# A two-layer graph attention network on one core: destination rows spread into PSUM by TensorE, lane numbers and softmax weights read from SBUF by VectorE

## The chip, the cores and the metric

The kernel runs on one core of one Trainium2 chip. The metric is the device time of one execution in microseconds (us), lower is better; the number quoted for a kernel is the median of several executions.

## What is computed

Two layers of graph attention over N = 3125 nodes with D = 128 features, E = 100,000 edges sorted by destination, H = 8 heads of 16, and a feed-forward network of width 512 after each attention. Cut to what matters:

```
for l in range(2):
    xn  = layernorm(x);  xp = xn + xn @ Wpos + bpos + deg * Wdeg + bdeg
    q, k, v = xp @ Wq + bq, xp @ Wk + bk, xp @ Wv + bv
    att = clip((q[dst] * k[src]).sum(head) / 4, -50, 50)      # one number per edge and head
    alpha = softmax of att over the edges (and the self loop) of each dst
    x = x + segment_sum(v[src] * alpha, dst) @ Wo + bo
    x = x + gelu(layernorm(x) @ W1 + b1) @ W2 + b2
out = layernorm(x_in + x)
```

## The kernel before

The nodes lie in 25 tiles of 128. The edges are cut into 99 groups a layer: 97 of 1024 edges (8 chunks of 128), and two short ones. Groups are worked from the last destinations to the first, so early groups can touch two tiles or more; a layer has 123 pairs of a group and a tile, 246 in both layers, against 198 groups. A group whose edges fall in two tiles is called doubled below. All five engines run the same loop over groups, each in its own program order, and meet through counting semaphores:

- **POOL** fetches the key and value rows of a group's source nodes, one indirect DMA a chunk (L561), into `kv`, which has 4 slots (`SLOTS`). Before group g it waits for `sum_begun` of the group that used the slot last. Its 8 gathers of a group are called a burst below.
- **SP** loads the destinations of each group, 1024 int32 broadcast to all 128 partitions (512 KB), into `dst_rows`, which has 3 slots (`ROWS`; L490). Before each it waits for `exp_done`.
- **ACT** makes the transposed one-hot matrix `hotT` of each pair, two groups ahead: `dist` = |destination - lane's node| from `dst_rows` (L697), `hotT` = relu(1 - dist) in bf16 (L700, which waits for `hotT_used`, posted by the gather's last matmul). It also takes the exponentials of the scores, once into `msg` (L706) and once more into the PSUM tile `shares` (L707). In its program the exponentials of group g stand ahead of the one-hots of group g + 2.
- **PE** (TensorE) gathers the queries of group g + 1 by `hotT` into PSUM banks 0 and 1: 24 bf16 matmuls for each pair (`gather_q`, L1332; it waits for `prod_done` of group g and `hotT_ready`). Then it sums the messages of group g by destination: 8 fp32 products for each pair, which the trace shows as 16 matmuls (`sum_pair`, L1350, into bank 2). The first product of a group posts `sum_begun`, the last of a pair `agg_done`.
- **DVE** (VectorE) makes `hot`, the one-hot matrix that is not transposed, from the destinations and 128 lane numbers in the PSUM tile `lanes` (L987), multiplies keys and queries (`prod`, L1069), sums them by head (`dots`, L1079), clips (L1081 to L1084), multiplies values by `shares` into `msg` (L1101), and adds each tile's sum to `acc` (L982).

In groups 36 to 83 of each layer the engines also carry out 24 "slots" of the feed-forward network, one for every two groups. The order on every engine is written out by hand; the number of pairs in a group is read at run time from `pair_tab`, and a loop (`Fori`) runs over them. PSUM has 8 banks: 0 and 1 hold the queries, 2 the sum, 3 `lanes`, 4, 5 and 6 the slots' tiles, 7 `shares`.

## Time and profile before

| what | us |
|---|---|
| median of 3 executions | 2742.39 |
| lowest and highest | 2732.53 and 2750.9 |
| the profiled execution | 2747.29 |
| its span in the trace | 2745.3 |
| busy in that span: PE, DVE, POOL, ACT | 1663.2, 1452.9, 1487.1, 912.1 |

The profile is a page for one execution (busy time of the engines, the chain of work that ended last, the costliest groups of instructions) and views of the trace that it was made from: groups by line with the idle time before them, the waits, and a timeline of instructions. In all of them "<-" behind an idle time names what released the instruction; "remote" is a semaphore whose poster the trace does not give, "issue" is time in which the engine waited for nothing that is shown.

### The profile page before, as it was taken

How to read it: one execution, taken by the hardware profiler on the slowest of the kernel's cores; microseconds unless marked ns; L12 is line 12 of the kernel's file. 1: busy time of each engine (PE TensorE's matmuls, PEld its weight loads, DVE VectorE, ACT ScalarE, POOL GpSimd, SP SyncE). 2: the span in 40 equal slices, each digit the busy share in tenths (PEclk: the TensorE clock that was granted, in tenths of full speed). 3: DMA queues.
4: the chain of work that ended last, by engine and by line, in shares of the span. 5: the costliest groups of instructions: out<-in, count | busy, mean ns of one | idle time of the engine just before them, and what ended most of it. 6: DMA issues, size and time to landing. Idle time of an engine off the chain costs nothing.

```text
span 2745.3 us, 44122 instructions
## 1 busy us (share of the span) xinstructions
PE 1663.2 (61%) x11693; PEld 1456.9 (53%) x11694; DVE 1452.9 (53%) x2484; ACT 912.1 (33%) x1616; POOL 1487.1 (54%) x1584
## 2 busy tenths in 40 slices
PE   7555555656666767666544565555656666665645
PEld 5454554555555656554533454555555555655644
DVE  9654444445555555555464444445455555555544
ACT  3223222223443444343232222222333443433422
POOL 0445555555555555556635555555655555655663
PEclk9668777667887777778566777767787777777776
DMA  2433334344433434444423333333433333443443
GB/s 67 132 108 121 112 109 125 115 121 122 125 115 116 127 115 127 124 123 141 132 79 104 120 106 119 117 117 120 131 119 119 117 117 117 123 128 117 129 136 93
DMA packets 120300, 322.97 MB, mean 118 GB/s; under 512 B 31459, under 2 KB 43684, under 8 KB 120170
## 3 DMA queue, kind: packets, MB, share of 16 engines
q0 software_dynamic: 75072, 205.10, 26.0%
q1 hardware_dynamic: 44292, 115.07, 12.5%
q10 hardware_dynamic: 838, 1.60, 0.2%
q8 instruction: 49, 0.80, 0.1%
q14 instruction: 49, 0.40, 0.0%
HBM read 313.45 MB, written 9.73 MB: 118 GB/s over the span
## 4 chain that ended last, share of the span: by engine, by line
DVE 25%; another core or an unknown queue 22%; issue 20%; PE 17%; DVEq 11%; ACT 3%; ACTq 1%; DMA 0%; SPq 0%
PE ps L1332 7%; PE ps L1350 6%; DVE dots L1079 6%; DVE prod L1069 5%; DVEq L354 4%; DVEq L388 3%; DVE hot L987 2%; DVE msg L1101 2%; DVE acc L982 1%; DVE q_parts L834 1%; DVEq L982 1%; DVE not_nan L1081 1%; DVEq L987 1%; ACT dist L697 1%
## 5 line engine op out<-in xcount | busy, mean ns | idle before, releaser
L561 POOL DMA_INDIRECT kv<-kv_tab,src_idx x1564 | 1483.3, 948 | 1230.9 <-PE ps L1350 541.0
L1350 PE MATMUL ps<-msg,hot 128*128 128x136 f32 x3896 | 764.3, 367 | 425.6 <-DVE acc L982 232.9
L1350 PEld LDWEIGHTS ps<-msg,hot 128*128 128x128 f32 x3896 | 705.6, 267 | 484.0 <-issue 298.0
L1332 PE MATMUL ps<-q_parts,hotT 128*128 x5844 | 560.0, 265 | 526.9 <-DVE prod L1069 228.5
L1332 PEld LDWEIGHTS ps<-q_parts,hotT 128*128 x5844 | 483.0, 121 | 610.7 <-issue 591.8
L1069 DVE TENSOR_TENSOR prod<-kv,ps 128x1024 f32<-128x1024 f32 (+1 forms) x198 | 238.2, 1203 | 362.1 <-remote 286.1
L987 DVE SCALAR_TENSOR_TENSOR hot<-dst_col,neg_base,ps 128x1024 f32<-128x1024 f32 (+1 forms) x246 | 311.7, 1267 | 126.1 <-issue 124.6
L700 ACT ACTIVATE hotT<-dist 128x1024 bf16 x246 | 259.9, 1057 | 331.2 <-remote 291.5
L697 ACT ACTIVATE dist<-dst_rows,neg_node 128x1024 bf16<-128x1024 int32 x246 | 282.5, 1148 | 153.0 <-issue 146.3
L1101 DVE TENSOR_TENSOR msg<-kv,ps 128x1024 f32<-128x1024 f32 (+1 forms) x198 | 238.7, 1205 | 105.5 <-issue 72.4
L706 ACT ACTIVATE msg<-att 128x64 f32<-128x64 f32 (+1 forms) x198 | 49.7, 251 | 625.9 <-DVE att L1084 468.9
L1079 DVE TENSOR_REDUCE dots<-prod 128x64 f32<-128x1024 f32 (+1 forms) x198 | 238.8, 1206 | 21.1 <-DVE prod L1069 14.9
L982 DVE TENSOR_TENSOR acc<-acc,ps 128x136 f32 x246 | 71.3, 290 | 295.4 <-PE ps L1350 166.2
L655 ACT ACTIVATE hid_slot<-ps,b1f 128x128 f32<-128x128 f32 x192 | 54.7, 368 | 309.5 <-PE ps L1303 201.4
L1303 PE MATMUL ps<-z1T,w1g 128*128 128x128 f32 x384 | 78.0, 356 | 52.1 <-issue 51.2
L1303 PEld LDWEIGHTS ps<-z1T,w1g 128*128 128x128 f32 x384 | 66.6, 255 | 63.1 <-issue 62.9
L638 ACT ACTIVATE spot<-spot,eps_col 128x1 f32<-128x1 f32 x100 | 29.0, 290 | 173.5 <-issue 92.8
L1019 DVE TENSOR_TENSOR x<-x,ps 128x128 f32<-128x128 f32 x26 | 7.4, 286 | 142.5 <-remote 110.4
L1309 PE MATMUL ps<-w,hid_slot 128*128 128x128 f32 x384 | 65.4, 325 | 16.1 <-ACT hid_slot L655 16.1
L1309 PEld LDWEIGHTS ps<-w,hid_slot 128*128 128x128 f32 x384 | 59.5, 236 | 18.7 <-ACT hid_slot L655 18.7
L667 ACT ACT_TABLE_LOAD x52 | 66.7, 1283 | 0.9
L664 ACT ACT_TABLE_LOAD x50 | 64.2, 1283 | 0.9
(215 smaller groups left out, 1000.8 us busy)
## 6 DMA issues: line engine op xcount, KB each, us to landing
dst_rows<-in_dst SPq DMA_DIRECT2D x194, 512.0 KB
kv<-kv_tab,src_idx POOLq DMA_INDIRECT x1564
kv_tab<-qkv SPq DMA_DIRECT2D x25, 128.0 KB
kv_tab<-qkv SPq DMA_DIRECT2D x3, 768.0 KB
out_tab<-z SPq DMA_DIRECT2D x24, 64.0 KB
out<-out_tab SPq DMA_DIRECT2D x1, 1498.5 KB
hot<-in_L_gnn_W SPq DMA_DIRECT2D x2, 256.0 KB
w<-in_L_gnn_W SPq DMA_DIRECT2D x2, 256.0 KB
```

The lines of the kernel that those rows point to most:

```text
L561: pool.indirect_dma_start(kv[:, u, c, :], None, kv_tab[l][:, :], bass.IndirectOffsetOnAxis(ap=src_idx[:, c, at(g)], axis=0)).then_inc(kv_i ...
L697: nc.scalar.activation(dist[:, :], dst_rows[:, r, :], ACT.Abs, bias=neg_node[:, at(t)]).then_inc(dist_done[l], 1)
L700: nc.scalar.activation(hotT[:, bass.ds(pr % 2, 1), :], dist[:, :], ACT.Relu, bias=1.0, scale=-1.0).then_inc(hotT_ready[l], 1)
L982: nc.vector.tensor_tensor(acc[:, at(t), :], acc[:, at(t), :], agg.unsqueeze(1), ALU.add).then_inc(evac_done[l], 1)
L987: nc.vector.scalar_tensor_tensor(out=hot[:, u % 2, 0:nch, :], in0=dst_col[:, 0:nch, at(g)].broadcast_to([P, nch, P]), scalar=neg_base[:, a ...
L1069: nc.vector.tensor_tensor(prod[:, 0:full].rearrange("p (c d) -> p c d", d=D), kv[:, u, 0:nch, 0:D], qd[:, 0:full].rearrange("p (c d) -> p ...
L1079: nc.vector.tensor_reduce(dots[:, 0:scores], prod[:, 0:full].rearrange("p (n d) -> p n d", d=HD), AX.X, ALU.add).then_inc(dot_done[l], 1)
L1101: nc.vector.tensor_tensor(half[:, 0:nch, 0:D].rearrange("p c (h d) -> p c h d", d=HD), kv[:, u, 0:nch, D:2 * D].rearrange("p c (h d) -> p ...
L1303: last = MM(banks["h"][c], w1g[:, l, c * P:(c + 1) * P], z1T[s], start=True, stop=True)
L1309: MM(banks["y"], hid[s][:, c * P:(c + 1) * P], w2[:, l, c, :], start=(c == 0), stop=False)
L1332: last = MM(qd[:, c * P:(c + 1) * P], hotT[:, bass.ds(pr % 2, 1), c * P:(c + 1) * P], q_parts[:, at(t), k * D:(k + 1) * D], start=first an ...
L1350: last = MM(agg, hot[:, u % 2, c, :], msg[:, u % 2, c, :], start=(c == 0), stop=(c == nch - 1))
```

## The change

The destinations no longer come as a broadcast of 512 KB. Once, at the start, ACT copies the table of destinations (99 rows of 1024) to bf16, POOL subtracts that from the table, which gives the rest as a second exact bf16 number, and SP stores both parts to a table in DRAM. For each group SP then loads 2 rows of bf16, 4 KB, into `part_rows` (4 slots). PE adds the two parts and spreads them over all partitions with two matmuls against a matrix of ones (`spread_row`, 2x128 by 2x512, one for each of the PSUM banks 3 and 4). It stands in PE's program after `gather_q` of group g + 1 and ahead of the sums, works for group g + 2, and waits for the row and for `dist_done` of all pairs of group g + 1, since the banks hold one row. ACT's `dist` reads the banks and waits for `rows_spread`.

DVE's `hot` reads the lane numbers from the SBUF tile that they were copied from, and `msg` takes the weights from the SBUF tile `msg` itself; the second exponential is gone. Both instructions now have two tensor inputs in SBUF, where they had one in SBUF and one in PSUM. The slots' tiles that lay in bank 4 move to bank 7.

```diff
-ROWS = 3
-TURN = 2 * ROWS
+ROWS = 4
+TURN = 6
...
-        dst_rows = sb("dst_rows", [P, ROWS, GE], I32)
+        dst_parts = sb("dst_parts", [NG, 2, GE], BF16)
+        part_rows = sb("part_rows", [2, ROWS, GE], BF16)
+        both = sb("both", [2, P], BF16)
...
-        lanes = ps[:, 3, 0:P]
-        shares = ps[:, 7, 0:GC * H].rearrange("p (c h) -> p c h", h=H)
+        spread_rows = ps[:, 3:5, :]
...
-                   "y": bank(6, P), "z2T": bank(4, P), "qkv": bank(4, 3 * D)}
+                   "y": bank(6, P), "z2T": bank(7, P), "qkv": bank(7, 3 * D)}
...
+            sp.wait_ge(parts_done, 2)
+            sp.dma_start(part_tab[:, :, :], dst_parts[:, :, :]).then_inc(parts_out, 16)
...
                     if g >= ROWS:
-                        sp.wait_ge(exp_done[l], max(1, g - ROWS))
+                        sp.wait_ge(rows_spread[l], g - ROWS + 1)
                     elif l:
-                        sp.wait_ge(exp_done[l - 1], NG)
-                    first, n = edges_of(g)
-                    sp.dma_start(dst_rows[:, r, 0:n], dst_d[first:first + n].partition_broadcast(P)).then_inc(rows_in[l][r], 16)
+                        sp.wait_ge(rows_spread[l - 1], NG)
+                    elif g == 0:
+                        sp.wait_ge(parts_out, 16)
+                    sp.dma_start(part_rows[:, r, :], part_tab[NG - 1 - g, :, :]).then_inc(rows_in[r], 16)
...
+            pool.memset(both[:, :], 1.0).then_inc(consts, 1)
+            pool.wait_ge(parts_done, 1)
+            nc.gpsimd.tensor_tensor(dst_parts[:, 1, :], dst_f, dst_parts[:, 0, :], ALU.subtract).then_inc(parts_done, 1)
...
+            act.wait_ge(src_rows, 2)
+            nc.scalar.activation(dst_parts[:, 0, :], dst_f, ACT.Copy).then_inc(parts_done, 1)
...
-                    act.wait_ge(rows_in[l][r], 16 * (n + 1))
+                    act.wait_ge(rows_spread[l], g + 1)
...
-                        nc.scalar.activation(dist[:, :], dst_rows[:, r, :], ACT.Abs, bias=neg_node[:, at(t)]).then_inc(dist_done[l], 1)
+                        nc.scalar.activation(dist[:, :].rearrange("p (b e) -> p b e", b=2), spread_rows, ACT.Abs, bias=neg_node[:, at(t)]).then_inc(dist_done[l], 1)
...
-                    nc.scalar.activation(msg[:, u % 2, 0:nch, D:MW], scores, ACT.Exp, scale=1.0 / SCALE)
-                    nc.scalar.activation(shares[:, 0:nch, :], scores, ACT.Exp, scale=1.0 / SCALE).then_inc(exp_done[l], 1)
+                    nc.scalar.activation(msg[:, u % 2, 0:nch, D:MW], scores, ACT.Exp, scale=1.0 / SCALE).then_inc(exp_done[l], 1)
...
-                link(nc.vector.tensor_copy(lanes, lane_row[:, :]))
...
-                                                   scalar=neg_base[:, at(t)], in1=spread(lanes, 1, nch),
+                                                   scalar=neg_base[:, at(t)], in1=spread(lane_row[:, :], 1, nch),
...
-                                            spread(shares[:, 0:nch, :], 3, HD), ALU.mult).then_inc(msg_done[l], 1)
+                                            spread(half[:, 0:nch, D:MW], 3, HD), ALU.mult).then_inc(msg_done[l], 1)
...
+                def spread_row(u, g, n, before):
+
+                    r = u % ROWS
+                    pe.wait_ge(rows_in[r], 16 * (l * rows_of_lane(r) + n + 1))
+                    if not (isinstance(g, int) and g == 0):
+                        pe.wait_ge(dist_done[l], before)
+                    for h in range(2):
+                        last = MM(spread_rows[:, h, :], both[:, :], part_rows[:, r, h * (GE // 2):(h + 1) * (GE // 2)], start=True, stop=True)
+                    last.then_inc(rows_spread[l], 1)
...
                     if more:
                         gather_q(u + 1, g + 1, word(d)[0], *word(d + 1))
+                    if more > 1:
+                        spread_row(u + 2, g + 2, i + (u + 2) // ROWS, word(d + 1)[0])
                     if not (isinstance(g, int) and g == 0):
                         sum_further(u + 1, g - 1, word(d - 2)[0], word(d - 1)[0])
...
+                if l == 0:
+                    pe.wait_ge(tab_ready, 1)
+                    spread_row(0, 0, 0, 0)
                 pe.wait_ge(q_part[2], l * NU + NU)
+                if l:
+                    spread_row(0, 0, 0, 0)
                 gather_q(0, 0, word(-1)[0], *word(0))
+                spread_row(1, 1, 0, word(0)[0])
```

On PE, between the gather of a group's queries and the sum, the program before reads (the end of the loop over a group's further tiles, then the first sum):

```order
L1332 MATMUL ps<-q_parts,hotT 128x128 x3
L1338 REGISTER_ALU
L1338 COMPARE_AND_BRANCH
L1337 UNCONDITIONAL_BRANCH
L1350 MATMUL ps<-msg,hot 128x136 [waits evac_done0,hot_done0,msg_done0]
L1350 MATMUL ps<-msg,hot 128x136 x7
```

and the changed program at the same place:

```order
L1357 MATMUL ps<-q_parts,hotT 128x128 x3
L1363 REGISTER_ALU
L1363 COMPARE_AND_BRANCH
L1362 UNCONDITIONAL_BRANCH
L1344 MATMUL ps<-part_rows,both 128x512 [waits dist_done0,rows_in2]
L1344 MATMUL ps<-part_rows,both 128x512
L1375 MATMUL ps<-msg,hot 128x136 [waits evac_done0,hot_done0,msg_done0]
L1375 MATMUL ps<-msg,hot 128x136 x7
```

The two matmuls at L1344 are the spreading of the row two groups on; they stand ahead of the sum of the current group. On ACT, from a group's exponentials to the one-hots of the second group after it, the program before reads:

```order
L706 ACTIVATE msg<-att 128x8x8 [waits att_done0]
L707 ACTIVATE ps<-att 128x64
L354 TENSOR_LOAD pair_tab
L354 ISA x2
L694 ISA [waits rows_in0_2]
L694 UNCONDITIONAL_BRANCH
L694 ISA
L697 REGISTER_ALU [waits hotT_ready0]
L697 REGISTER_ALU
L697 ISA
L697 ACTIVATE dist<-dst_rows,neg_node 128x1024
L700 ISA [waits hotT_used0,dist_done0]
```

and the changed program:

```order
L723 ACTIVATE msg<-att 128x8x8 [waits att_done0]
L359 TENSOR_LOAD pair_tab
L359 ISA x2
L711 ISA [waits rows_spread0]
L711 UNCONDITIONAL_BRANCH
L711 ISA
L714 REGISTER_ALU [waits hotT_ready0]
L714 REGISTER_ALU
L714 ISA
L714 ACTIVATE dist<-ps,neg_node 128x1024
L717 ISA [waits hotT_used0,dist_done0]
L717 ACTIVATE hotT<-dist 128x1024
```

The wait at the head of the one-hots is for PE (`rows_spread`) where it was for a DMA (`rows_in`), and the activation into PSUM is gone.

## Rows read from the trace of the kernel before

**Rows 1.** The page's chain that ended last, share of the span by engine.
```profile
DVE 25%; another core or an unknown queue 22%; issue 20%; PE 17%; DVEq 11%; ACT 3%; ACTq 1%; DMA 0%; SPq 0%
```
**Rows 2.** The page's costliest groups: out<-in xcount | busy us, mean ns | idle before.
```profile
L561 POOL DMA_INDIRECT kv<-kv_tab,src_idx x1564 | 1483.3, 948 | 1230.9 <-PE ps L1350 541.0
...
L1069 DVE TENSOR_TENSOR prod<-kv,ps 128x1024 f32<-128x1024 f32 (+1 forms) x198 | 238.2, 1203 | 362.1 <-remote 286.1
L987 DVE SCALAR_TENSOR_TENSOR hot<-dst_col,neg_base,ps 128x1024 f32<-128x1024 f32 (+1 forms) x246 | 311.7, 1267 | 126.1 <-issue 124.6
L700 ACT ACTIVATE hotT<-dist 128x1024 bf16 x246 | 259.9, 1057 | 331.2 <-remote 291.5
L697 ACT ACTIVATE dist<-dst_rows,neg_node 128x1024 bf16<-128x1024 int32 x246 | 282.5, 1148 | 153.0 <-issue 146.3
```
**Rows 3.** Timeline of a steady group, layer 0: start us, us, engine, line, [idle before].
```profile
1363.17 0.94 POOL L561 DMA_INDIRECT kv<-kv_tab,src_idx  x1 [2.17 <-remote]
...
1364.71 2.80 PE L1332 MATMUL ps<-q_parts,hotT 128*128 x24 [3.86 <-DVE prod L1069]
...
1366.71 1.22 DVE L1101 TENSOR_TENSOR msg<-kv,ps 128x1024 f32<-128x1024 f32 x1 [0.72 <-ACT ps L707]
1366.92 0.95 POOL L561 DMA_INDIRECT kv<-kv_tab,src_idx  x1 [0.30 <-issue]
...
1368.05 1.27 DVE L987 SCALAR_TENSOR_TENSOR hot<-dst_col,neg_base,ps 128x1024 f32<-128x1024 f32 x1
...
1368.28 3.97 PE L1350 MATMUL ps<-msg,hot 128*128 128x136 f32 x16 [0.77 <-DVE acc L982]
...
1371.92 0.95 POOL L561 DMA_INDIRECT kv<-kv_tab,src_idx  x1 [0.30 <-issue]
1374.67 1.22 DVE L1069 TENSOR_TENSOR prod<-kv,ps 128x1024 f32<-128x1024 f32 x1 [5.34 <-remote]
1374.94 0.94 POOL L561 DMA_INDIRECT kv<-kv_tab,src_idx  x1 [2.08 <-remote]
```
**Rows 4.** Timeline at the start of layer 1, ACT.
```profile
1469.10 1.06 ACT L700 ACTIVATE hotT<-dist 128x1024 bf16 x1 [23.09 <-remote]
```
**Rows 5.** Timeline at the end of layer 0, POOL, around the 4-chunk group.
```profile
1390.52 0.95 POOL L561 DMA_INDIRECT kv<-kv_tab,src_idx  x1 [0.30 <-issue]
...
1392.92 0.94 POOL L561 DMA_INDIRECT kv<-kv_tab,src_idx  x1 [1.46 <-PE ps L1350]
```
**Rows 6.** Timeline between the layers: gathers beside DVE operations with two SBUF inputs.
```profile
1439.23 0.82 DVE L961 TENSOR_TENSOR q_parts<-acc,q_parts  x1 [0.72 <-issue]
1439.63 1.24 POOL L561 DMA_INDIRECT kv<-kv_tab,src_idx  x1 [0.30 <-issue]
...
1442.13 0.82 DVE L967 TENSOR_TENSOR acc<-qkv,acc  x1 [2.07 <-issue]
1442.43 1.35 POOL L561 DMA_INDIRECT kv<-kv_tab,src_idx  x1 [0.30 <-issue]
```
**Rows 7.** Timeline of a doubled group, layer 0.
```profile
389.18 5.25 PE L1332 MATMUL ps<-q_parts,hotT 128*128 x47 [5.54 <-ACT hotT L700]
...
394.82 0.22 PE L1332 MATMUL ps<-q_parts,hotT 128*128 x1 [0.39 <-issue]
...
396.37 0.95 POOL L561 DMA_INDIRECT kv<-kv_tab,src_idx  x1 [0.30 <-issue]
...
399.40 1.06 ACT L700 ACTIVATE hotT<-dist 128x1024 bf16 x1 [6.59 <-remote]
...
404.28 0.94 POOL L561 DMA_INDIRECT kv<-kv_tab,src_idx  x1 [6.97 <-PE ps L1350]
```
**Rows 8.** Groups by line: the second exponential, its reader, and wide bf16 matmuls.
```profile
L1101 DVE TENSOR_TENSOR msg<-kv,ps 128x1024 f32<-128x1024 f32 (+1 forms) x198 | 238.7, 1205 | 105.5 <-issue 72.4 <-ACT ps L707 32.6
...
L707 ACT ACTIVATE ps<-att 128x64 f32<-128x64 f32 (+1 forms) x198 | 41.2, 208 | 0.0
...
L1285 PE MATMUL ps<-q_parts,zeros 128*128 128x384 bf16 x48 | 14.6, 461 | 3.8 <-issue 3.8
```

More of the change, by code:

```diff
@@ L256, in gnn_program @@
         hot_used = sem("hot_used")
-        rows_in = [sems(f"rows_in{l}_", ROWS) for l in range(L)]
+        rows_in = sems("rows_in", ROWS)
+        rows_spread = sems("rows_spread")
+        parts_done = sem("parts_done")
+        parts_out = sem("parts_out")
         dst_away = sem("dst_away")
@@ L342, in gnn_program @@
         block = ctx.enter_context(nc.Block())
-        NCONST = 14
+        NCONST = 15
         RAW_LOADS = 16
@@ L712, in _, with edge_group @@
                 word = pair_words(act, 0)
-                one_hots(word, 0, 0, 0)
+                one_hots(word, 0, 0)
                 if l == 0:
                     fold_kept(1)
-                one_hots(word, 1, 1, 0)
-                def edge_group(word, d, g, u, r, n, slot=None):
+                one_hots(word, 1, 1)
+                def edge_group(word, d, g, u, slot=None):
                     even, odd = (slot is not None and u % 2 == k for k in (0, 1))
@@ L752, in _ @@
                     for u in range(TURN):
-                        edge_group(word, u, TURN * i + u, u, (u + 2) % ROWS, TURN // ROWS * i + (u + 2) // ROWS, slot=number + u // 2)
+                        edge_group(word, u, TURN * i + u, u, slot=number + u // 2)
                 word = pair_words(act, 0)
                 for g in range(2 * SLOT_END, NG):
-                    edge_group(word, g, g, g, (g + 2) % ROWS, (g + 2) // ROWS, slot=slot_at(g))
+                    edge_group(word, g, g, g, slot=slot_at(g))
                 start = tail_start(act)
@@ L1364, in tail_biases, with pe_group @@
                     MM(in_tail["y"], ones[0:1, :], b2_row[:, l, :], start=True, stop=False)
-                def pe_group(u, g, word, d, more=True, slot=None):
+                def pe_group(u, g, i, word, d, more=2, slot=None):
                     even, odd = (slot is not None and u % 2 == k for k in (0, 1))
@@ L1401, in _ @@
                     for u in range(SLOTS):
-                        pe_group(u, SLOTS * i + u, word, u)
+                        pe_group(u, SLOTS * i + u, i, word, u)
                 word = pair_words(pe, 0)
                 for g in range(2 * FIRST_SLOT, 2 * FIRST_SLOT + SLOTS):
-                    pe_group(g % SLOTS, g, word, g, slot=slot_at(g))
+                    pe_group(g % SLOTS, g, g // SLOTS, word, g, slot=slot_at(g))
                 with pe.Fori(2 * FIRST_SLOT // SLOTS + 1, 2 * SLOT_END // SLOTS) as i:
@@ L1409, in _ @@
                     for u in range(SLOTS):
-                        pe_group(u, SLOTS * i + u, word, u, slot=number + u // 2)
+                        pe_group(u, SLOTS * i + u, i, word, u, slot=number + u // 2)
                 word = pair_words(pe, 0)
                 for g in range(2 * SLOT_END, 2 * SLOT_END + SLOTS):
-                    pe_group(g % SLOTS, g, word, g, slot=slot_at(g))
+                    pe_group(g % SLOTS, g, g // SLOTS, word, g, slot=slot_at(g))
                 with pe.Fori(2 * SLOT_END // SLOTS + 1, NG // SLOTS) as i:
@@ L1416, in _ @@
                     for u in range(SLOTS):
-                        pe_group(u, SLOTS * i + u, word, u)
+                        pe_group(u, SLOTS * i + u, i, word, u)
                 word = pair_words(pe, 0)
                 for g in range(NG // SLOTS * SLOTS, NG):
-                    pe_group(g % SLOTS, g, word, g, more=g < NG - 1)
+                    pe_group(g % SLOTS, g, g // SLOTS, word, g, more=NG - 1 - g)
                 sum_further(NG - 1, NG - 1, word(NG - 2)[0], word(NG - 1)[0])
```

15 lines of the change are left out of this document (9 added, 6 removed).

## The prediction

> **What bounds the kernel now.** I read the chain that ended last first. It gives no engine more than a quarter: 25% VectorE, 22% "another core or an unknown queue", 20% issue, 17% PE [rows 1]. So several engines take turns around one loop, and semaphores whose poster is not shown hold it for a fifth of the time. Next I read the costliest groups for who waits [rows 2]: POOL's gathers are busy 1483.3 us and stood idle for 1230.9 before them, 541.0 of it for the sum on PE; `prod` waited 286.1 and `hotT` 291.5 for "remote". Then the timeline of one steady group, which shows what the loop is [rows 3]. POOL's burst begins at 1363.17 and its last gather at 1371.92, 8.75 us later. PE gathers queries at 1364.71 and sums from 1368.28 to 1372.25. Yet `prod`, which waits for the gather that was recorded by 1367.51, starts at 1374.67, and the next burst, which waits for the first product of a sum, starts at 1374.94. Both come 2.75 and 3.02 us after the burst's last issue. I read this as: while POOL issues a burst, PE's completions are not passed on; they arrive together some 1.8 us after the last gather ended. The start of layer 1 says the same without a row load under way: `hotT` waited 23.09 us for a gather recorded long before [rows 4]. The period, 1374.94 - 1363.17 = 11.77 us, is therefore a burst of 8.75 plus 3.02, and PE's and ACT's work is free as long as it ends inside it. A longer burst is paid in full.
>
> In a doubled group this cover is gone [rows 7]. PE runs 47 of the gather's 48 matmuls by 394.43, then single ones, while POOL still issues; the burst's last issue is at 396.37, the posts come at 399.40, and the next burst starts at 404.28, 7.91 us after the last issue instead of 3.02. There are 246 - 198 = 48 further pairs in the two layers, from the counts of `hot` and `prod` [rows 2].
>
> **The change part by part**, on the profiled execution (2747.29 us, 4.9 above the median).
>
> *VectorE's two operands in SBUF.* I expect no gain for VectorE: the instruction's element count stays. The loss is on POOL. Before, `msg` runs from 1366.71 to 1367.93 with one input in PSUM; a gather starts in the middle of it and still takes 0.95 [rows 3]. Where the operation beside it has two SBUF inputs, it is different [rows 6]: the gather that starts at 1439.63, inside L961 (1439.23 to 1440.05), takes 1.24, which is 0.95 counted from 0.13 before L961's end; the one at 1442.43, inside L967 (1442.13 to 1442.95), takes 1.35, by the same rule to 0.01. So a gather waits for the end of such an operation. In the steady group the gather at 1366.92 would wait for `msg` until 1367.80, 0.88 us, and the next, moved from 1368.17 to 1369.05, for `hot` (1368.05 to 1369.32) until 1369.19, 0.14: 1.02 us per burst, as an upper end 198 x 1.02 = +202. In other groups the two operations fall partly behind the burst; by the same two steps for each burst of the timeline, 325 of the 444 operations (246 + 198) hold the start of a gather, at 0.42 us on average: +136, my value. Lower end 0, if a gather needs the port only outside these pieces.
>
> A sentence of the Trainium skill bears on this from both sides: the page "SBUF — State Buffer", section "Who interferes with whom", states that a VectorE instruction with two SBUF inputs contends with a GpSimd instruction that reads SBUF, and one with at most one does not. By that the trace agrees, 1.24 and 1.35 against 0.95. The same section infers that descriptor generation needs only the write side, so that `tensor_tensor` would not stall a gather; by that the term were 0, and the two long gathers speak against it. It is a rival below.
>
> *The row's way over PE.* `dist` of group g + 2 may now start only when PE's post has arrived. In a steady group it arrives with the others at 1374.67: `dist` 1.15 and `hotT` 1.06 [rows 2] with 0.3 between end at 1377.2, and `prod`, for which the next gather waits too, at 1375.89 [rows 3]; of the 1.3 between I take half, 0.7, as the gather's delay, since PE needs a while after `prod` too. Behind it stand two matmuls of 512 columns. Their price: 24 matmuls of 128 columns took 2.80 [rows 3], 0.117 each, so 0.47 for 512 columns; L1285's 384 columns at 461 ns [rows 8] make 0.61 for 512, the upper end. Two cost 0.93. The sum would end 1.6 later, at 1373.9, and the posts come at 1374.7 + 1.0 for the longer burst: still hidden, 0.
>
> In a doubled group it is not hidden. The second pair's `dist` and `hotT` too stand behind the post, and the exponential of the group waits behind them on ACT's queue, with `msg` and the sum behind that. I take 0.7 for the late gather and 0.93 for the two matmuls: 1.6 us, 48 x 1.6 = +77. Lower end 0 (the trickle of single matmuls hides it); upper end two pairs' one-hots in full, 2 x 2.2 = 4.4, 48 x 4.4 = +211.
>
> In the 96 groups with slots (48 a layer) PE also has the feed-forward matmuls, and I take half of the two matmuls as exposed: 96 x 0.45 = +43, between 0 and 96 x 0.93 = +89. The slots' tiles that move to bank 7 cost nothing: `shares` is gone from it.
>
> *The second exponential.* 198 at 208 ns are 41.2 us, and `msg` waited 32.6 for it [rows 8]. `msg` starts earlier by less than its 0.21, and in steady groups only hidden work is shortened. I take half, -20, between -41 and 0.
>
> *Row loads.* 194 broadcasts of 512 KB go (97 whole groups a layer), 4 KB come. If that traffic were part of what delays the posts, the short burst at the layer's end, where no load is under way, bounds it: from its last issue at 1390.52 to the next burst at 1392.92 are 2.40 us [rows 5] against 3.02 in rows 3, so at most 198 x 0.62 = -123. Rows 4 show the long hold without any load, so I take 0.
>
> *Starts of the layers and prologue.* The first one-hots were ready before the posts came; now `spread`, `dist`, `hotT`, gather come after them, about 2.2 + 2.8 = 5 us a layer: +10, between 0 and +20. The table's copy, subtraction and store lie beside the preparation of nodes and tables and get no term of their own.
>
> Sum: 136 + 77 + 43 - 20 + 0 + 10 = +246. 2747.3 + 246 = 2993; less 4.9 for the median, 2988.
>
> **Rivals.**
> *Only the bursts count.* The chain over PE and ACT stays hidden in doubled and slot groups as well. For it: PE's single matmuls at the end of a burst are waiting time that extra work may fill. Against it: 7.91 us from the last issue to the next burst in a doubled group, with PE busy. Then 136 - 20 + 10 = +126: 2868.
> *No price at the port.* The page's inference holds for gathers, and the long ones of rows 6 have another cause. Then 77 + 43 - 20 + 10 = +110: 2852.
> *The loads were part of the hold* (the other side). Without 194 x 512 KB = 99 MB of writes into SBUF the posts come earlier after each burst. At 0.62 us a burst it is -123 and, with the chain then hidden, +126 - 123 = +3: 2745, no change; if the hold vanished, 1.8 us a burst, 198 x 1.8 = -356 and 2742 + 126 - 356 = 2512. It decides the sign from 0.64 us a burst on, 126 / 198. For it: the short burst of rows 5. Against it: rows 4, and that the short burst's sum starts late for its own reasons.
> *The chain cascades.* Port at the steady group's 1.02 (+202), doubled groups at 3 us (+144), slot groups at 0.93 (+89), -20 and +10: +425, 3167.
>
> **How the numbers follow.** Chances: forecast 0.50, only the bursts 0.20, no price at the port 0.07, loads 0.11, cascade 0.12. The first two rivals lie near each other and inside the range; the forecast's own range is 2900 to 3080. From 2810 to 3110 leaves out the loads' case and half of the cascade, some 0.18. A measurement of this kernel tells about 1% from no change. The loads' case I split into 0.07 faster and 0.04 within 1%; all others are slower by more, 0.89.
>
> **What would show it.** Port: mean time of a gather 0.948 [rows 2] rises to about 1.035 (136 / 1564 = 0.087), with single gathers of 1.1 to 1.9 that start inside `msg` or `hot`, and bursts of 9.2 to 9.8 instead of 8.75. Chain: `dist` idle before it for "remote" or PE, where it was 153.0 mostly issue; a doubled group some 2 us longer; gather matmuls that wait for `hotT`. Steady groups: period 12.8 instead of 11.77. VectorE's `msg` and `hot` keep 1205 and 1267 ns; if they became longer, VectorE and not POOL pays for the port, and the bursts would stay 8.75. The forecast is wrong if bursts stay at 8.75, if the posts come less than 2.4 us after a burst's last issue, or if steady groups too run longer than the burst explains.

## The result: 1.7% slower, not 9%

The changed kernel took 2788.8 us (median of 4, 2782.1 to 2802.0) where the kernel before took 2746.1 beside it (median of 4). The ratio is 1.0168, with a 95% interval from 1.0142 to 1.0193. The forecast was 2988 with a range from 2810 to 3110: the sign was right, the size was nearly six times too large, and the time lies below the range.

The profile after. The page's chain that ended last, share of the span by engine:

```profile
another core or an unknown queue 24%; PE 24%; issue 22%; DVE 13%; ACT 9%; DVEq 6%; ACTq 3%; DMA 0%; SPq 0%
```

Its costliest groups, columns as in [rows 2]:

```profile
L576 POOL DMA_INDIRECT kv<-kv_tab,src_idx x1564 | 1605.6, 1027 | 1141.2 <-PE ps L1375 497.0
...
L714 ACT ACTIVATE dist<-ps,neg_node 128x1024 bf16<-128x1024 f32 x246 | 273.9, 1113 | 1101.9 <-remote 754.3
L1002 DVE SCALAR_TENSOR_TENSOR hot<-dst_col,neg_base,lane_row 128x1024 f32<-128x1024 f32 (+1 forms) x246 | 313.0, 1272 | 235.1 <-issue 127.8
...
L1116 DVE TENSOR_TENSOR msg<-kv,msg 128x1024 f32<-128x1024 f32 (+1 forms) x198 | 240.4, 1214 | 114.9 <-issue 73.6
...
L1344 PE MATMUL ps<-part_rows,both 2*128 2x512 bf16 x396 | 161.2, 492 | 48.4 <-issue 26.8
```

Much of this stands as the prediction had it. The gather rose from 948 ns [rows 2] to 1027, which is 1605.6 - 1483.3 = 122 us more on POOL (136 was forecast). `hot` and `msg` keep their length, 1272 and 1214 against 1267 and 1205, so it is POOL that waits at the port, not VectorE. The wide matmul takes 492 ns, against my 0.47 us. And `dist`, which had waited 153.0 us before [rows 2], now waits 1101.9, mostly for a post of PE. Yet the idle time ahead of the gathers fell by 90 us, from 1230.9 to 1141.2: what the port added to the bursts was taken from the gaps between them.

The timeline of a steady group of the changed kernel shows how:

```profile
1321.13 0.94 POOL L576 DMA_INDIRECT kv<-kv_tab,src_idx  x1 [2.03 <-remote]
...
1324.75 1.23 DVE L1116 TENSOR_TENSOR msg<-kv,msg 128x1024 f32<-128x1024 f32 x1 [0.25 <-issue]
1324.88 1.91 POOL L576 DMA_INDIRECT kv<-kv_tab,src_idx  x1 [0.30 <-issue]
...
1330.85 0.94 POOL L576 DMA_INDIRECT kv<-kv_tab,src_idx  x1 [0.30 <-issue]
1332.85 1.22 DVE L1084 TENSOR_TENSOR prod<-kv,ps 128x1024 f32<-128x1024 f32 x1 [4.50 <-remote]
1333.17 0.95 POOL L576 DMA_INDIRECT kv<-kv_tab,src_idx  x1 [1.38 <-remote]
```

The gather at 1324.88 starts inside `msg` and takes 1.91 us; the last issue is 9.72 us after the first instead of 8.75. But `prod` starts 11.72 us after the first issue, where it was 1374.67 - 1363.17 = 11.50 [rows 3], and only 2.00 us after the last one, where it was 2.75; less than 2.4 was one of the prediction's own signs of being wrong. The posts did not move with the end of the burst. I had read a fixed distance from the last issue out of bursts that all had the same length, and from those the first issue fits just as well. The start of layer 1 in the trace of before had the answer. There four bursts run one behind the other; the first and the last of their 32 gathers:

```profile
1423.64 0.94 POOL L561 DMA_INDIRECT kv<-kv_tab,src_idx  x1 [28.53 <-DMA kv_tab<-qkv]
...
1464.09 0.95 POOL L561 DMA_INDIRECT kv<-kv_tab,src_idx  x1 [0.30 <-issue]
```

The post came at 1469.10 [rows 4]. That is 5.0 us after the last issue, not 2.75 to 3.02, and 45.5 us after the first, 1.42 for each of 32 gathers; 11.50 for 8 gathers are 1.44 each. I call this theory S: the posts wait for some work that takes 1.43 us a gather from the first issue on, so POOL's issues, 1.25 apart, have slack. Theory P is the prediction's: the posts come at a fixed distance from the last issue.

Where the 43 us lie in these two traces is seen by cutting both at `prod` of groups 4, 36, 84 and 96 of each layer. Of before, the rows read: stretch, its length, then busy time of PE, PEld, DVE, ACT and POOL, PE's granted clock, DMA share, GB/s.

```profile
193.24:613.61 420.37, 239.83 (x1771) 217.90 (x1772) 199.83 (x284) 108.91 (x152) 233.79 (x249) 0.73 0.39 117
613.61:1256.91 643.30, 428.99 (x2911) 369.90 (x2909) 354.91 (x661) 260.57 (x511) 362.72 (x384) 0.76 0.40 122
1256.91:1393.34 136.43, 76.77 (x503) 67.36 (x504) 70.29 (x105) 35.68 (x60) 86.81 (x93) 0.67 0.43 128
1524.33:1944.70 420.37, 239.89 (x1771) 217.72 (x1772) 199.64 (x283) 108.91 (x152) 233.83 (x249) 0.74 0.39 117
1944.70:2579.53 634.83, 407.13 (x2844) 359.64 (x2843) 348.68 (x662) 256.07 (x487) 362.45 (x383) 0.76 0.40 122
```

The same stretches of the changed kernel:

```profile
200.76:645.27 444.51, 264.98 (x1841) 217.81 (x1840) 200.80 (x283) 102.12 (x120) 254.67 (x249) 0.72 0.25 74
645.27:1284.73 639.46, 459.31 (x3004) 370.91 (x3003) 357.12 (x660) 247.98 (x459) 391.10 (x383) 0.76 0.29 84
1284.73:1422.65 137.92, 81.87 (x517) 64.35 (x516) 70.81 (x103) 33.42 (x49) 97.25 (x92) 0.69 0.31 91
1553.99:1998.76 444.77, 267.73 (x1840) 223.13 (x1840) 200.69 (x283) 102.29 (x120) 252.84 (x249) 0.70 0.26 74
1998.76:2622.66 623.90, 452.53 (x2934) 373.13 (x2934) 350.57 (x661) 243.42 (x437) 395.52 (x383) 0.74 0.29 83
```

Groups 4 to 35, without feed-forward slots, grew by 24.1 and 24.4 us. Groups 36 to 83, with slots, shrank by 3.8 and 10.9, although PE has 30 and 45 us more to do in them. The steady groups 84 to 95 grew by 1.5 in layer 0 and by 0.1 in layer 1. Of the rest, some 8 us, 7.5 lie ahead of `prod` of group 4 of layer 0 (200.76 against 193.24), although POOL's first gather starts no later there (86.28 against 86.53); the start of layer 1 grew by 0.4. A second pair of traces, in experiment 2, puts the cost elsewhere, so this table doesn't place it.

### The profile page after: what moved, and what is told of

The parts are those of the page before. It is cut to its first block, busy times and chain, and to the rows that moved or that the text cites. A ratio compares the mean times of both kernels' runs of the same rounds, so it can differ in the third digit from the quotient of the medians.

```text
span 2788.9 us, 44946 instructions
## 1 busy us (share of the span) xinstructions
PE 1817.7 (65%) x12089; PEld 1480.0 (53%) x12090; DVE 1460.3 (52%) x2482; ACT 871.6 (31%) x1419; POOL 1611.7 (58%) x1586
## 4 chain that ended last, share of the span: by engine, by line
another core or an unknown queue 24%; PE 24%; issue 22%; DVE 13%; ACT 9%; DVEq 6%; ACTq 3%; DMA 0%; SPq 0%
PE ps L1357 10%; PE ps L1375 8%; ACT dist L714 4%; DVE dots L1094 3%; DVE prod L1084 2%; DVEq L359 2%; PE ps L1344 2%; ACT hotT L717 2%; DVE q_parts L850 1%; ACTq L359 1%; DVE hot L1002 1%; PE ps L1318 1%; DVE msg L1116 1%; DVEq L397 1%
## 5 line engine op out<-in xcount | busy, mean ns | idle before, releaser
L576 POOL DMA_INDIRECT kv<-kv_tab,src_idx x1564 | 1605.6, 1027 | 1141.2 <-PE ps L1375 497.0
L1357 PE MATMUL ps<-q_parts,hotT 128*128 x5844 | 585.8, 271 | 570.0 <-issue 277.0
L1375 PE MATMUL ps<-msg,hot 128*128 128x136 f32 x3896 | 754.6, 364 | 246.4 <-DVE acc L997 138.0
L1375 PEld LDWEIGHTS ps<-msg,hot 128*128 128x128 f32 x3896 | 691.1, 262 | 369.5 <-issue 231.3
L1357 PEld LDWEIGHTS ps<-q_parts,hotT 128*128 x5844 | 500.9, 123 | 662.9 <-issue 643.3
L714 ACT ACTIVATE dist<-ps,neg_node 128x1024 bf16<-128x1024 f32 x246 | 273.9, 1113 | 1101.9 <-remote 754.3
L1002 DVE SCALAR_TENSOR_TENSOR hot<-dst_col,neg_base,lane_row 128x1024 f32<-128x1024 f32 (+1 forms) x246 | 313.0, 1272 | 235.1 <-issue 127.8
L1116 DVE TENSOR_TENSOR msg<-kv,msg 128x1024 f32<-128x1024 f32 (+1 forms) x198 | 240.4, 1214 | 114.9 <-issue 73.6
L1344 PE MATMUL ps<-part_rows,both 2*128 2x512 bf16 x396 | 161.2, 492 | 48.4 <-issue 26.8
L1344 PEld LDWEIGHTS ps<-part_rows,both 2*128 2x128 bf16 x396 | 25.3, 99 | 87.5 <-issue 81.3
```

The source lines that it names most:

```text
L576: pool.indirect_dma_start(kv[:, u, c, :], None, kv_tab[l][:, :], bass.IndirectOffsetOnAxis(ap=src_idx[:, c, at(g)], axis=0)).then_inc(kv_i ...
L714: nc.scalar.activation(dist[:, :].rearrange("p (b e) -> p b e", b=2), spread_rows, ACT.Abs, bias=neg_node[:, at(t)]).then_inc(dist_done[l], 1)
L1002: nc.vector.scalar_tensor_tensor(out=hot[:, u % 2, 0:nch, :], in0=dst_col[:, 0:nch, at(g)].broadcast_to([P, nch, P]), scalar=neg_base[:, a ...
L1116: nc.vector.tensor_tensor(half[:, 0:nch, 0:D].rearrange("p c (h d) -> p c h d", d=HD), kv[:, u, 0:nch, D:2 * D].rearrange("p c (h d) -> p ...
L1344: last = MM(spread_rows[:, h, :], both[:, :], part_rows[:, r, h * (GE // 2):(h + 1) * (GE // 2)], start=True, stop=True)
L1357: last = MM(qd[:, c * P:(c + 1) * P], hotT[:, bass.ds(pr % 2, 1), c * P:(c + 1) * P], q_parts[:, at(t), k * D:(k + 1) * D], start=first an ...
```

## The experiments

Each experiment was timed in turn with the kernel before on the same chip, and the ratios are to that. The time of the kernel before was not the same in all sets of runs, and this turned out to be the main finding: in two sets (that of experiment 2 with the repetition of experiment 1 and the long pause of experiment 4, and the last run of experiment 6) it took 2669 to 2671 us, in all others 2100 to 2105; beside the changed kernel's first measurement it had been 2746. One chip showed both, 2671 in one set and 2100 in a later one, so it is not a property of the chip alone. The two conditions are told apart by the trace, below, and I call them "held" (2669 to 2746 for the kernel before, which the prediction and the result are about) and "not held" (2100).

**Experiment 1: VectorE's two SBUF operands alone, on the kernel before.**

```diff
-                                                   scalar=neg_base[:, at(t)], in1=spread(lanes, 1, nch),
+                                                   scalar=neg_base[:, at(t)], in1=spread(lane_row[:, :], 1, nch),
...
-                                            spread(shares[:, 0:nch, :], 3, HD), ALU.mult).then_inc(msg_done[l], 1)
+                                            spread(half[:, 0:nch, D:MW], 3, HD), ALU.mult).then_inc(msg_done[l], 1)
...
-                    nc.scalar.activation(msg[:, u % 2, 0:nch, D:MW], scores, ACT.Exp, scale=1.0 / SCALE)
-                    nc.scalar.activation(shares[:, 0:nch, :], scores, ACT.Exp, scale=1.0 / SCALE).then_inc(exp_done[l], 1)
+                    nc.scalar.activation(msg[:, u % 2, 0:nch, D:MW], scores, ACT.Exp, scale=1.0 / SCALE).then_inc(exp_done[l], 1)
```

> The kernel before with only VectorE's part of the change: hot and msg read two SBUF operands, the second exponential and the copy of the lane numbers are gone; rows still come by the 512 KB broadcast. Theory P (the prediction's: the posts come about 3.0 us after a burst's last issue, so a longer burst is paid in full): gathers of 1.03 us on average, bursts of about 9.4, and +136 - 20 = +116, about 2860. Theory S (formed on the trace of after: the posts come about 11.5 us after a burst's FIRST issue, 1.43 us for each of 8 gathers, however late the last is issued): the same gathers and bursts, but the time between burst start and prod stays 11.5 to 11.7 in steady groups, and the kernel is within 1% of before, 2725 to 2775.

Measured: 2234.5 us against 2105.3, ratio 1.0626 (1.0598 to 1.0654), +129 us. Neither theory had said that before would take 2105. The difference is near theory P's +116, but not for P's reason: no post is held here, POOL simply issues without a pause, and what it pays is the longer gathers (1618.9 us of them, against 1484.7 in experiment 3, whose gathers are those of before). So this set doesn't decide between P and S. The same edit in a held set:

> The kernel before with VectorE's two SBUF operands alone, again, beside the changed kernel. Without hold: +129 as in the first set, and the changed kernel within 5 us of it. With hold: 0 to +15, and the changed kernel 30 to 50 above it.

Measured: 2669.5 against 2669.5, ratio 1.000 (0.997 to 1.003). So one edit costs 129 us or nothing, and which of the two depends on the condition. P's +116 is refuted for the held condition. The other half of S's expectation, `prod` 11.5 to 11.7 us after a burst's first issue, came true only in part. I take the 24 steady groups 84 to 95 of both layers. In this held trace `prod` starts 11.3 to 12.1 us after the first issue in 9 of them, and in 12 it starts before the burst's last issue; in the first profile of before these were 23 and 1, in the changed kernel 11 and 8. So with stalls inside the bursts some posts get through before a burst is over, which S as I put it did not have. The gathers are long in both. The page's row for them, not held and then held:

```profile
L561 POOL DMA_INDIRECT kv<-kv_tab,src_idx x1564 | 1618.9, 1035 | 580.6 <-issue 468.9
```
```profile
L561 POOL DMA_INDIRECT kv<-kv_tab,src_idx x1564 | 1604.8, 1026 | 1001.2 <-issue 428.3
```

1035 and 1026 ns, against 948 before. Not held, POOL's idle time is 580.6, and 468.9 of it is the 0.30 us between two gathers, so hardly anything is left to take a longer gather from, and the chain that ended last is POOL's:

```profile
POOL 65%; issue 21%; PE 5%; DVE 5%; DMA 3%; DVEq 1%; ACT 0%; ACTq 0%; POOLq 0%; SPq 0%
```

The timeline of one group, not held, with the stall that the prediction described:

```profile
1063.03 1.22 DVE L1099 TENSOR_TENSOR msg<-kv,msg 128x1024 f32<-128x1024 f32 x1 [1.07 <-ACT msg L706]
1063.24 1.84 POOL L561 DMA_INDIRECT kv<-kv_tab,src_idx  x1 [0.30 <-issue]
1064.38 1.28 DVE L985 SCALAR_TENSOR_TENSOR hot<-dst_col,neg_base,lane_row 128x1024 f32<-128x1024 f32 x1
...
1065.38 1.10 POOL L561 DMA_INDIRECT kv<-kv_tab,src_idx  x1 [0.30 <-issue]
```

By the prediction's rule the first should end 0.95 after 1064.12 (the end of `msg` less 0.13), at 1065.07, and it ends at 1065.08; the second starts in `hot`, which ends at 1065.66, and ends at 1066.48, 0.95 after 1065.53.

**Experiment 2: the kernel before and the changed kernel in one held set.**

> The kernel before itself, with a profile. In the first set of experiments it took 2105 us, in the measurement behind the prediction 2746. If this run takes about 2105, the posts of PE that VectorE and POOL wait for come within 1 us of the matmul's end and POOL gathers without a pause (period of a steady group 10.0 us); if about 2746, they come 11.5 us after a burst's first issue, as in the profile shown.

> The changed kernel itself beside before. Where before takes about 2105 (no hold of the posts): the port is paid in full and the row's way over PE is hidden, +125 to +135, 2230 to 2240. Where before takes about 2746 (hold): +40 to +50, as measured first.

Measured: before 2667.4 (ratio 0.9991), after 2709.8, ratio 1.0146 (1.0118 to 1.0174), +40. With experiment 1 in the same set, whose interval reaches to 1.003, this leaves all or nearly all of it to the row's way over PE.

The two traces, cut at the same groups as the first pair, don't place the cost where the first pair did. Growth from before to after, us:

| groups | first pair | this pair |
|---|---|---|
| 4 to 35, layer 0 and layer 1 | +24.1, +24.4 | -0.5, +11.5 |
| 36 to 83 (slots), layer 0 and layer 1 | -3.8, -10.9 | +18.8, +11.2 |
| 84 to 95, layer 0 and layer 1 | +1.5, +0.1 | -2.0, +1.4 |
| all the rest | +8.2 | -1.2 |
| whole span | +43.6 | +39.1 |

Groups 4 to 35 run the same work in both layers, and yet they took 409.6 and 423.5 us in this one execution of the changed kernel. The sum of +40 us is repeatable; what a stretch of one trace adds to it is not.

 `prod` of before, held, again waits for "remote" (297.8 us). Not held, this is what stands in the waits of the kernel with small row loads (experiment 3), whose instructions are those of before:

```profile
DVE prod L1072 <- DMA kv<-kv_tab,src_idx: 187.8, 93, 7.0
```

and its timeline:

```profile
1043.88 1.22 DVE L1072 TENSOR_TENSOR prod<-kv,ps 128x1024 f32<-128x1024 f32 x1 [3.59 <-DMA kv<-kv_tab,src_idx]
...
1045.71 2.44 PE L1335 MATMUL ps<-q_parts,hotT 128*128 x24 [2.50 <-DVE prod L1072]
...
1052.25 0.94 POOL L564 DMA_INDIRECT kv<-kv_tab,src_idx  x1 [0.31 <-issue]
1053.50 0.95 POOL L564 DMA_INDIRECT kv<-kv_tab,src_idx  x1 [0.30 <-issue]
1053.89 1.22 DVE L1072 TENSOR_TENSOR prod<-kv,ps 128x1024 f32<-128x1024 f32 x1 [3.25 <-DMA kv<-kv_tab,src_idx]
```

Gathers run without a gap, 1.25 us apart, through the boundary of two groups; `prod` waits for the gathered data and not for PE, and the period is 1053.89 - 1043.88 = 10.01 us, 8 x 1.25, where the held one is 11.8.

**Experiment 3: the traffic of the row loads.** The kernel before; after the first three groups each load fills one partition only, so the one-hots are made from old destinations.

```diff
-                    sp.dma_start(dst_rows[:, r, 0:n], dst_d[first:first + n].partition_broadcast(P)).then_inc(rows_in[l][r], 16)
+                    if l == 0 and g < ROWS:
+                        sp.dma_start(dst_rows[:, r, 0:n], dst_d[first:first + n].partition_broadcast(P)).then_inc(rows_in[l][r], 16)
+                    else:
+                        sp.dma_start(dst_rows[0:1, r, 0:n], dst_d[first:first + n].partition_broadcast(1)).then_inc(rows_in[l][r], 16)
```

> The kernel before with only the traffic of the row loads gone: after the first three groups of layer 0 each load brings 4 KB to one partition instead of 512 KB to 128, so the one-hots are made from old destinations in 127 partitions (values differ, the instructions and waits are the same). If the loads are part of what holds PE's posts: up to 0.62 us less a burst, -123, about 2620. If they are no part of it (theories P and S both): within 0.5% of before, 2733 to 2760.

Measured: 2104.7 against 2105.3, ratio 0.9999 (0.9989 to 1.0009). The 99 MB cost nothing where posts are not held. This set could not test whether they lengthen a hold; against that speaks that the changed kernel, without them, still holds its posts for 11.6 to 11.8 us in 11 of the 24 steady groups.

**Experiment 4: POOL's gathers further apart.** The kernel before, with a memset behind every gather.

```diff
                         pool.indirect_dma_start(kv[:, u, c, :], None, kv_tab[l][:, :],
                                                 bass.IndirectOffsetOnAxis(ap=src_idx[:, c, at(g)], axis=0)).then_inc(kv_in[l][u], 16)
+                        pool.wait_ge(paused, pauses[0])
+                        pool.memset(pause[:, :], 0.0).then_inc(paused, 1)
+                        pauses[0] += 1
```

> The kernel before with a small memset on POOL behind each of the 1564 gathers, which spaces them by about 0.2 us more (1.45 instead of 1.25 start to start, a burst of about 10.2 instead of 8.75), and touches no operand of the others. Theory P: the posts still come 3.0 us after the last issue, 1.4 us later in each of 198 bursts: +280, about 3025. Theory S: the posts stay at 11.5 us after the burst's first issue as long as 8 x spacing is under 11.4: between 0 and +60, 2746 to 2806.

Measured, not held: 2152.6, ratio 1.0223 (1.0206 to 1.024), +47. The memset of 128x64 took 0.17 us, but most of it fell into the 0.30 that was idle anyway: 1.286 us start to start, 0.035 more, times 1564 is 55. A longer one in a held set:

> The kernel before with a memset of 128x200 instead of 128x64 behind each gather, some 0.1 to 0.3 us more between gathers than x4 (which had 1.286 start to start against 1.251 and took 47 us more). Without hold every 0.1 us of spacing costs 156 us in 1564 gathers. With hold, theory S (posts 11.5 us after the first issue): no more than +60 for a spacing up to 1.43; theory P (posts 3.0 us after the last issue): 7 x 198 = 139 us for each 0.1 us.

Measured, held: 2657.7 against 2669.5, ratio 0.9946 (0.9919 to 0.9973). This speaks against P once more. Gathers were 1.40 us apart and a burst 9.8 us long instead of 8.77; by theory P that is 1.03 x 198 = +204 us, and the kernel became 0.5% faster. That it became faster at all S did not say either. Its timeline:

```profile
1274.95 0.95 POOL L564 DMA_INDIRECT kv<-kv_tab,src_idx  x1 [0.17 <-issue]
1276.98 1.22 DVE L1075 TENSOR_TENSOR prod<-kv,ps 128x1024 f32<-128x1024 f32 x1 [6.74 <-remote]
1277.27 0.95 POOL L564 DMA_INDIRECT kv<-kv_tab,src_idx  x1 [1.08 <-remote]
...
1285.10 1.22 DVE L1075 TENSOR_TENSOR prod<-kv,ps 128x1024 f32<-128x1024 f32 x1 [1.20 <-remote]
1285.68 0.95 POOL L564 DMA_INDIRECT kv<-kv_tab,src_idx  x1 [0.17 <-issue]
1287.09 0.96 POOL L564 DMA_INDIRECT kv<-kv_tab,src_idx  x1 [0.17 <-issue]
```

The first `prod` comes 2.03 us after the burst's last issue, 11.83 after its first (1265.15); the second comes in the middle of a burst, 7.83 after its first issue. So posts do get through during a burst when the gathers are 1.40 apart: `prod` starts before the last issue in 12 of the 24 steady groups. By S as put, with 1.43 a gather, they should still have waited for 11.4. A possible reading is that a post gets through whenever the work has caught up with the gathers issued so far, which gathers 1.40 apart, or a stall inside a burst, would allow; no run tests it.

**Experiment 5: a pause in the middle of the burst.** The kernel before, with three memsets of 128x256 behind the fourth gather of each group.

> The kernel before with three memsets of 128x256 on POOL behind the fourth gather of each group, a pause of about 1.2 us in the middle of the burst, 196 in all. If POOL's time between gathers lets PE's posts through (hold): prod and the sums start earlier in some groups, and the kernel is between 0.97 and 1.00 of before although POOL has some 235 us more to do. If the hold lasts until the burst is over, whatever lies between: 1.00 to 1.08. Without hold POOL pays it in full, +200 to +260, 1.10 to 1.12 of 2105.

Measured, not held: 2232.8 against 2099.6, ratio 1.0635 (1.0617 to 1.0653), +133. The pause added 0.68 us (1.94 from the fourth gather's start to the fifth's, where it is 1.25 without a pause), not 1.2, and it is paid in full: 196 x 0.68 = 133. What it does to held posts stays untried.

**Experiment 6: the one-hots' wait for PE taken away.** The changed kernel; both spreading matmuls go to bank 3 except in a layer's first group, and `dist` reads bank 4 twice, an old row.

```diff
-                    act.wait_ge(rows_spread[l], g + 1)
+                    if isinstance(g, int) and g == 0:
+                        act.wait_ge(rows_spread[l], g + 1)
...
-                        nc.scalar.activation(dist[:, :].rearrange("p (b e) -> p b e", b=2), spread_rows, ACT.Abs, bias=neg_node[:, at(t)]).then_inc(dist_done[l], 1)
+                        nc.scalar.activation(dist[:, :].rearrange("p (b e) -> p b e", b=2), old_row, ACT.Abs, bias=neg_node[:, at(t)]).then_inc(dist_done[l], 1)
...
-                        last = MM(spread_rows[:, h, :], both[:, :], part_rows[:, r, h * (GE // 2):(h + 1) * (GE // 2)], start=True, stop=True)
+                        last = MM(spread_rows[:, h if isinstance(g, int) and g == 0 else 0, :], both[:, :], part_rows[:, r, h * (GE // 2):(h + 1) * (GE // 2)], start=True, stop=True)
```

> The changed kernel with all its instructions, but both spreading matmuls of all rows except the first go to bank 3, and dist reads bank 4 twice and waits for PE in the first group of a layer only; the one-hots are made from an old row (values differ). What goes is only the wait of the one-hots for PE's post. If that wait is what the change costs (the one-hots behind the held posts, in groups with two tiles above all): 35 to 55 us less than after, 2735 to 2755. If the two matmuls or VectorE's operands are what it costs: within 10 us of after, 2780 to 2800.

Measured, not held: 2232.7, ratio 1.0598 (1.0577 to 1.0619). This is experiment 1's cost and nothing more: not held, the matmuls are hidden under the gathers, and the wait has nothing left to cost. Three repetitions, with these expectations, came in the same condition:

> The changed kernel without the wait of the one-hots for PE's post (both spreading matmuls go to bank 3, dist reads an old row in bank 4), again. On a chip that holds PE's posts (before about 2670 to 2750) the changed kernel is 1.015 times before and VectorE's operands alone 1.000. If the wait is what is left: 0.995 to 1.003 of before. If the two matmuls are: 1.01 to 1.02. On a chip without hold (before about 2105): 1.06 again, which tells nothing new.

> The changed kernel without the one-hots' wait for PE, once more. On a chip that holds PE's posts: 0.995 to 1.003 of before if the wait is what is left of the cost, 1.01 to 1.02 if the two matmuls are. Without hold: 1.063.

> The changed kernel without the one-hots' wait for PE, once more, in the hope of a chip that holds PE's posts. There: 0.995 to 1.003 of before if the wait is what is left of the cost, 1.01 to 1.02 if the two matmuls are. Without hold: 1.062.

Measured: 1.0627, 1.0618 and 1.0624. The fourth was held:

> The changed kernel without the one-hots' wait for PE's post, again for a chip that holds the posts. There: 0.995 to 1.003 of before if the wait is what is left of the cost, 1.01 to 1.02 if the two matmuls are. Without hold: 1.062.

Measured, held: 2686.2 against 2671.4, ratio 1.0064 (1.0044 to 1.0085), +15. It lies between the two answers. The wait is 1.0146 or 1.0168 less 1.0064, 0.8 to 1.0%, some 22 to 28 us (the runs with and without it come from different chips, each against before on its own); 0.6%, some 17 us, is left for the two matmuls and the rest. The waits of the changed kernel as measured first, and of this one:

```profile
ACT dist L714 <- remote: 754.3, 103, 21.3
...
PE ps L1357 <- ACT hotT L717: 257.1, 75, 23.4
```
```profile
ACT hotT L719 <- remote: 188.9, 48, 16.0
...
PE ps L1359 <- ACT hotT L719: 76.6, 31, 5.8
```

PE's gather waited 257.1 us for `hotT` in the changed kernel (209.9 in that of experiment 2, the nearer comparison) and 76.6 without the wait. The kernel became only some 25 us shorter, so most of the difference was not on the path that ends last.

**Experiment 7: one matmul of the two, and the spreading ahead of the gather.** The first leaves the second half of a row old in all but a layer's first two groups; the second swaps two calls in `pe_group`.

```diff
-                    for h in range(2):
+                    for h in range(2 if isinstance(g, int) and g < 2 else 1):
```
```diff
-                    if more:
-                        gather_q(u + 1, g + 1, word(d)[0], *word(d + 1))
                     if more > 1:
                         spread_row(u + 2, g + 2, i + (u + 2) // ROWS, word(d + 1)[0])
+                    if more:
+                        gather_q(u + 1, g + 1, word(d)[0], *word(d + 1))
```

> The changed kernel with one of the two spreading matmuls in every group but the first two of a layer (the second half of dist's row stays old). If the matmuls' time is what is left with hold: half of the 1.5% goes, 1.005 to 1.010. If the wait: 1.012 to 1.018 of before, as the changed kernel. Without hold: 1.06.

> The changed kernel with spread_row of group g + 2 ahead of gather_q of group g + 1 instead of behind it, so that its post stands ahead of 24 or 48 matmuls and may get through earlier. If the one-hots' wait for that post costs with hold: less than the changed kernel, 0.99 to 1.01 of before. If the matmuls cost: unchanged, 1.015, or more, since they now delay the gather too. Without hold: 1.06, as the gathers bound.

> The changed kernel with spread_row ahead of gather_q, once more. With hold: 0.99 to 1.01 of before if the wait is what costs, 1.015 or more if the matmuls do. Without hold: 1.061.

> The changed kernel with spread_row ahead of gather_q. On a chip that holds PE's posts, where the changed kernel was 1.015 to 1.017 of before and the one without the wait 1.006: if the post gets through earlier when fewer matmuls stand ahead of it, 1.000 to 1.010; if it is held all the same, 1.013 to 1.02. Without hold: 1.061.

Measured, not held in all four: 1.0627, and 1.0613, 1.0624, 1.0628. Neither shows anything beyond experiment 1's cost; for the held condition both stay untried, and with them whether an earlier post would get through.

**Experiment 8: the lane numbers alone from SBUF.** `hot` has two SBUF operands, `msg` and both exponentials are as before.

> The kernel before with only the lane numbers read from SBUF (hot with two SBUF operands; msg and both exponentials as before). Without hold: 246 operations of 1.27 us instead of 444, so a little over half of the port's price, +60 to +90, 1.03 to 1.043 of 2100. With hold: 0.995 to 1.005.

Measured, not held: 2206.6 against 2100.7, ratio 1.0497 (1.0479 to 1.0515), +106, above the +60 to +90 expected. `hot` alone makes 106 of the 129 us, more than its 246 of 444 operations. In this trace 226 gathers start inside a `hot`, and the gathers together take 1599.9 us, 115 more than in experiment 3. My share by count was too low; why the two operations together stall less than their sum was not tested, and stalls that push the next gather past the other operation are the likely reason.

## Why the prediction was wrong

*The reading of the bound* failed, in one sentence: "they arrive together some 1.8 us after the last gather ended ... A longer burst is paid in full." That POOL's burst and PE's posts are tied was right for the run shown, and that the hold was there without row loads too. What was wrong is the end of it that I tied it to: the port's stalls, 136 us of POOL's time, were priced as 136 us of the kernel's, and what experiment 1 shows in the same condition is no cost. Experiment 1 has the port's stalls at 1.000, and experiment 4 has bursts 1.03 us longer at 0.995 of the time. In the held condition gathers can stand 0.15 us further apart without any cost.

*The port term*, +136, was right as a count of POOL's time: 122 us in the changed kernel and 136 in experiment 1 (1618.9 - 1483.3). Where POOL bounds, experiment 1 cost +129, so there the term is nearly paid in full, and the exponential's -20 doesn't show. The stall rule gave the ends of the two gathers worked out there to 0.01 us. The Trainium skill's page "SBUF — State Buffer", section "Who interferes with whom", infers that descriptor generation needs only the write side and that `tensor_tensor` does not stall it; gathers of 1.84 us behind a `msg` of 1.22 speak against that inference, while its rule on two SBUF inputs agrees. The rival "no price at the port" (2852) would have come nearer than the forecast, though still 63 us too long, and for the wrong reason: the port had its price in POOL's time, and the held loop did not pay it.

*The row's way over PE* was too large as a whole: doubled groups +77, slot groups +43 and layer starts +10 make +130, and experiment 2 measured +40 beside a port that cost nothing. The mechanism exists: experiment 6 takes 0.8 to 1.0%, 22 to 28 us, away with the wait alone. How it divides between doubled and slot groups is not shown. In the first pair of traces, groups 4 to 35, with 13 doubled groups a layer, grew by 24.1 + 24.4 = 48.5 us, 1.9 us for each of 26, near my 1.6; in the second pair by 11.0, 0.4 each. One doubled group in the changed kernel, where 48 gather matmuls and then the two spreading ones stand ahead of the post:

```profile
315.67 0.69 PE L1357 MATMUL ps<-q_parts,hotT 128*128 x5 [0.44 <-issue]
316.29 1.03 PE L1344 MATMUL ps<-part_rows,both 2*128 2x512 bf16 x2
317.83 1.11 ACT L714 ACTIVATE dist<-ps,neg_node 128x1024 bf16<-128x1024 f32 x1 [13.73 <-PE ps L1344]
318.26 3.96 PE L1375 MATMUL ps<-msg,hot 128*128 128x136 f32 x16 [0.94 <-issue]
```

`dist` waits 13.73 us for PE and the sum follows only after the spreading.

*Slot groups*, +43 ("I take half of the two matmuls as exposed"): with their 18 doubled groups they should have grown by 43 + 18 x 1.6 = 72 us. They came out 14.7 us shorter in the first pair, although PE had 30 and 45 us more to do there, and 30.0 longer in the second. Both are far below 72, so most of what PE had more to do went into its own idle time; more than that the two pairs don't settle.

*The second exponential* at -20 and the *layer starts* at +10 were measured by no run alone. The first pair has +7.5 ahead of group 4 of layer 0 and +0.4 at the start of layer 1, where I had 5 each; the second pair has -3.3 and -0.1. *Row loads* at 0 were right where they could be tested.

The range was too narrow below: I had kept 0 as the port's lower end, but only for gathers that miss the port's busy pieces; that the stalls happen and are hidden had no chance of its own. The trace shown held two explanations of 2.75 us, and the second needed only a division by the number of gathers.

No version beats the kernel before in both conditions: the long pause of experiment 4 gains 0.5% held, the short one loses 2.2% not held, and nothing else was clearly faster than before in either.

## What to carry to other kernels

When a wait ends at a fixed distance from something, check the distance against an instance of another length before pricing a change of that length; here one row, four bursts in a chain, would have done. Keep one operand of a long VectorE instruction in PSUM when GpSimd issues indirect DMAs beside it: reading both from SBUF cost nothing here where POOL had slack and 6% where it had not. Cut a second pair of traces at the same places before saying where in a kernel a small difference lies. And time a kernel in more than one set of runs before sizing a change: the same edit was worth 0 and 129 us.

## What the runs showed of the hardware that I had not expected

The same program ran at 2100 to 2105 us and at 2669 to 2746 us, the two apart by 27 to 31%, and one chip showed both at different times. What the traces show to differ is the arrival of PE's posts. In the held condition they often arrive about 1.43 us for each gather issued after a burst's first issue, in [rows 7] PE goes on with single matmuls after 47, and the granted clock of the profiled runs was 0.72 to 0.77. Not held, POOL issues without a gap and the clock was 0.80 to 0.83. What holds the posts stays open, and so does whether the clock has a part in it. The gathers' own lengths are the same in both conditions (951 ns held in the kernel before, 949 not held in experiment 3), and so is the time until a gather's last packet ends, 2.44 and 2.41 us after its issue (medians), so the gathered rows don't come later.

A VectorE operation with two SBUF inputs delayed a gather that started inside it to 0.13 us before its end. With `hot` alone, 226 gathers were met that way, and the kernel became 106 us longer.
